# Six of the eight weight blocks of a shared expert's second half computed with seven block products instead of eight

## The reference

```
g, u   = split(x @ w_sh_gate_up)        # 512 -> 2 x 1024
shared = (silu(g) * u) @ w_sh_down      # 1024 -> 512
out    = layernorm(x + routed + shared)
```

## Time and profile before

| | us |
|---|---|
| median of 3 runs (lowest, highest) | 689.05 (688.68, 689.08) |
| the profiled execution's own time | 688.28 |
| its span | 686.5 |
| busy PE / DVE / ACT / POOL | 666.1 / 425.4 / 294.3 / 294.3 |

### The profile page before, as it was taken

The page is one execution under the profiler, slowest core; times in us unless marked ns, Lnnn a source line. Parts: engine busy times, 40 slices in busy tenths (PEclk is TensorE's granted clock), DMA queues, the critical chain, the costliest instruction groups (busy, mean ns, idle before and its releaser), DMA issues.

```text
span 686.5 us, 16409 instructions
## 1 busy us (share of the span) xinstructions
PE 666.1 (97%) x6828; PEld 531.9 (77%) x6828; DVE 425.4 (62%) x745; ACT 294.3 (43%) x510; POOL 294.3 (43%) x308
## 2 busy tenths in 40 slices
PE   9999999999999999999999999999999999999994
PEld 7767777677777777787887888888887888888883
DVE  5875865876844464488946544554456267676655
ACT  5343444455454432531023656655667442142232
POOL 0747567667645431011015335533552244726232
PEclk9999999999999999999999999999999999999998
DMA  8213234232642441100064478676748765414222
GB/s 286 83 35 86 76 98 106 88 112 57 175 138 75 129 141 33 46 0 1 21 231 157 140 292 295 214 220 255 216 153 271 229 218 159 123 66 131 65 78 92
DMA packets 65998, 92.47 MB, mean 135 GB/s; under 512 B 16960, under 2 KB 32064, under 8 KB 65920
## 3 DMA queue, kind: packets, MB, share of 16 engines
q1 hardware_dynamic: 60240, 72.76, 32.2%
q0 software_dynamic: 5680, 18.62, 9.4%
HBM read 67.56 MB, written 23.79 MB: 133 GB/s over the span
## 4 chain that ended last, share of the span: by engine, by line
PE 67%; DVE 14%; POOL 8%; issue 6%; ACT 4%; DMA 1%; POOLq 0%; DVEq 0%; ACTq 0%
PE zbank L1181 8%; PE wbank L1181 7%; PE bank L1305 7%; PE bank L1194 7%; PE bank L1073 7%; PE zbank L1268 6%; PE wbank L1268 6%; PE bank L1128 4%; DVE x L1464 3%; PE zbank L1281 2%; PE bank L1181 2%; PE wbank L1107 2%; PE zbank L1091 2%; POOL za L1758 2%; DVE sg L1454 1%
## 5 line engine op out<-in xcount | busy, mean ns | idle before, releaser
L1790 POOL TENSOR_TENSOR xl<-RAW,xh 128x1024 fp32r<-128x1024 f32 x23 | 55.4, 2407 | 121.1 <-ACT xh L1657 120.9
L1673 ACT ACTIVATE ah<-sg 128x512 fp32r<-128x512 f32 x48 | 30.3, 632 | 157.4 <-DVE sg L1454 157.4
L1803 POOL DMA_INDIRECT xg<-x1d,idxu x39 | 42.1, 1079 | 71.2 <-DVE idxu L889 41.3
L1444 DVE TENSOR_TENSOR GL<-RAW,GH 128x1024 fp32r<-128x1024 f32 x42 | 50.3, 1223 | 11.2 <-ACT GH L1652 9.8
L1456 DVE TENSOR_TENSOR al<-sg,ah 128x512 fp32r<-128x512 f32 x48 | 34.2, 712 | 33.5 <-ACT ah L1673 33.5
L1194 PE MATMUL bank<-xh,ah 128*128 128x512 f32 x128 | 51.3, 401 | 2.3 <-DVE x L1464 1.9
L1828 POOL DMA_INDIRECT xg<-yd,SI x32 | 35.8, 1120 | 40.0 <-DVE x L1512 23.6
L1194 PE MATMUL bank<-xh,al 128*128 128x512 f32 x128 | 50.0, 390 | 0.0
L1194 PE MATMUL bank<-xl,ah 128*128 128x512 f32 x128 | 49.9, 390 | 0.0
L1073 PE MATMUL bank<-xh,GH 128*128 128x512 f32 x112 | 47.9, 427 | 0.8 <-DVE kS L1346 0.8
L1454 DVE TENSOR_TENSOR sg<-sg,zbank 128x512 f32<-128x512 f32 x22 | 15.1, 685 | 53.4 <-PE zbank L1268 36.4
(11 more groups left out here) (301 smaller groups left out, 1753.6 us busy)
## 6 DMA issues: line engine op xcount, KB each, us to landing
RAW<-in_wgu SPq DMA_DIRECT2D x13, 1024.0 KB, 5.8
yd<-RAW SPq DMA_DIRECT2D x39, 256.0 KB, 5.2
RAW<-in_wsgu SPq DMA_DIRECT2D x14, 512.0 KB, 4.8
RAW<-in_wd SPq DMA_DIRECT2D x13, 512.0 KB, 5.8
xr<-in_xT SPq DMA_DIRECT2D x16, 256.0 KB, 4.7
x<-in_xtok SPq DMA_DIRECT2D x16, 256.0 KB, 4.2
x1d<-x SPq DMA_DIRECT2D x16, 256.0 KB, 2.5
RAW<-in_wsd SPq DMA_DIRECT2D x8, 512.0 KB, 4.5
```

The lines of the kernel that those rows point to most:

```text
L1444: e.tensor_tensor(GL[:, w % 2, k:k + 2, :], gate_raw(w, k), GH[:, w % 2, k:k + 2, :].bitcast(F32), ALU.subtract).then_inc(*mark("low", "g" ...
L1790: e.tensor_tensor(DL[:, w % 2, :, :], draw[:, raw_of(w), :, :], DH[:, w % 2, :, :].bitcast(F32), ALU.subtract).then_inc(*mark("low p", "d" ...
L1803: e.indirect_dma_start(place(s), None, x1d, bass.IndirectOffsetOnAxis(ap=idxu[:, LINES[s]:LINES[s] + 1], axis=0)).then_inc(*mark(f"dma xg{ ...
```

## The change

A unit half `fc` for the quarters 2 and 3 together is a product of a 2 x 2 block matrix of weights (gate and up; lower and upper half of the contraction) with a 2 x 2 block matrix of tokens (lower and upper half of the contraction; quarter 2 and quarter 3). The change computes six of the eight such products, numbered b = 2 to 7 (units BASE + 1 to BASE + 3), in Winograd's form of Strassen's method: seven block products of 6 matmuls each in place of eight. The two of unit BASE stay as they were.

The seven products need four sums of weight blocks for every b (`mix sums`, GpSimd, 128x256 each) and four sums of token blocks (`pair sums`, `pair more`: VectorE, 128x1024 each), all split into high and low again (`mix high`, `mix low`, `pair split`). The results are put together in PSUM: products accumulate onto each other, with three bank copies on ScalarE (`copy 1`, `copy 5`, `copy 2`) and two additions on VectorE (`add 5`, `add 7`) per b. PE's order in a block is 1, 5, 6, 2, 7, 3, 4, with four groups of a down (6 matmuls each) of the block before in between. Banks 0 to 3 are all in use by one block; the next one takes them over. The token fetch of quarter 3 is issued one job earlier than before, quarter 2 is fetched a second time (`fetch pair`), the routing's scratch memory is shared with it, and the last downs are (3, 3) and then (3, 2), with tiles 12 to 15 and 8 to 11 finished in these.

```diff
+SEVEN = {1: (0, "B11", 0, True), 2: (1, "B21", 0, False), 3: (6, "B22", 1, False), 4: (2, "T4", 2, False),
+         5: (3, "T1", 3, True), 6: (4, "T2", 1, False), 7: (5, "T3", 2, False)}
...
+    def mix(b, after):
+        do("mix sums", b, after)
+        do("mix high", b, after)
+        do("mix high sums", b)
+        do("mix low", b)
+    def block(b, order):
+        w, fc = BASE + b // 2, b % 2
+        for p in order:
+            do("mul", b, p, left[SEVEN[p][2]] if SEVEN[p][3] else None)
+            mul_end[b] = ("mul", b, p)
+            if p == 1:
+                do("copy 1", b, left[1])
+            elif p == 5:
+                do("copy 5", b)
+            elif p == 6:
+                do("copy 2", b, left[2])
+                do("add 5", b)
+            elif p == 2:
+                do("silu 2", b)
+                left[0] = ("silu", w, 2, fc)
+            elif p == 7:
+                do("add 7", b)
+            elif p == 3:
+                do("pair act", b, 3, ("down", w - 2, 3, 3) if b > 3 else None)
+                left[1], left[3] = ("silu", w, 3, fc), ("low", "a", w, 3, fc)
+            elif p == 4:
+                do("pair act", b, 2, ("down", w - 1, 2, 3))
+                left[2] = ("low", "a", w, 2, fc)
+            yield p
...
+        if j == JOBS - 3:
+            do("fetch pair")
+        if j == JOBS - 2:
+            do("fetch tokens", 3, ("gate", 4 + j, "r", 0, 1), range(4))
+        if j == JOBS - 1:
+            do("pair sums")
-        if j == JOBS - 1:
-            do("fetch tokens", 3, row_left[1], range(4))
...
-    seq = [(BASE + n, q) for n, q in ((0, 2), (0, 3), (1, 2), (1, 3), (2, 2), (3, 2), (2, 3), (3, 3))]
...
+    do("pair more", gate_end[4 + JOBS - 1])
+    rows_down(JOBS - 1, iter(()))
+    mix(2, gate_end[4 + JOBS - 1])
     do("fetch", 0)
     do("fetch", 1)
+    for step, _ in enumerate(first, 2):
+        if step < 6:
+            do("fetched high", 3, step - 2)
+            do("fetched low", 3, step - 2)
+    do("pair split", "T2", None)
+    split_down(BASE + 1)
+    do("load down", BASE + 2)
+    for step, _ in enumerate(gate(BASE, 3)):
+        if step % 2 == 0:
+            join(step // 2)
+    do("pair split", "T3", gate_end[BASE])
+    do("pair split", "T4", None)
+    join(4)
+    side = {(2, 3): "j5", (2, 4): "j6", (3, 1): "f0", (3, 3): "j7", (3, 4): "j8", (4, 1): "f1", (4, 5): "f2", (4, 3): "j9", (4, 4): "j10",
+            (5, 1): "f3", (5, 5): "f4", (5, 3): "j11", (5, 4): "j12", (6, 1): "f5", (6, 5): "f6", (6, 3): "j13", (6, 4): "j14",
+            (7, 1): "f7", (7, 3): "j15"}
+    for b in range(2, 8):
+        u = b // 2
+        downs = pair_down(u - 1, 2 + b % 2)
+        for p in block(b, (1, 5, 6, 2, 7, 3, 4)):
+            if p == 1 and b < 7:
+                after = mul_end[b - 1] if b > 2 else gate_end[BASE]
+                do("mix sums", b + 1, after)
+                do("mix high", b + 1, after)
+                if b in (4, 6):
+                    split_down(BASE + u)
+            if p == 2 and b < 7:
+                do("mix high sums", b + 1)
+                do("mix low", b + 1)
+            if p in (1, 3):
                 scale()
+            if (b, p) in side:
+                kind, i = side[b, p][0], int(side[b, p][1:])
+                (join if kind == "j" else finish)(i)
+            if p in (6 if b % 2 == 0 else 5, 2) or p in (3, 4) and b < 7:
+                next(downs, None)
+        if b == 2:
             do("load gate", BASE + 3)
             do("load down", BASE + 3)
+    scale()
+    for _ in downs:
+        pass
+    for i in pair_down(3, 3):
+        finish(i)
+        scale(keep=1)
+    for i in pair_down(3, 2):
...
+                elif step == "mul":
+                    b, p, free = a
+                    s, name, to, opens = SEVEN[p]
+                    if free:
+                        e.wait_ge(*on(*free))
+                    if p in (1, 2):
+                        e.wait_ge(*on("low", "m", b, 0))
+                    elif p == 4:
+                        e.wait_ge(*on("low", "m", b, 2))
+                    else:
+                        e.wait_ge(*on("low p", "m", b))
+                    if b == 2:
+                        e.wait_ge(*(on("low", "pair", name) if name[0] == "T" else on("low", "f", 3 if name == "B22" else 2, 3)))
+                    if p == 6:
+                        e.wait_ge(*on("copied", b, 1))
+                    elif p == 2:
+                        e.wait_ge(*on("copied", b, 1))
+                    elif p == 7:
+                        e.wait_ge(*on("copied", b, 2))
+                    elif p == 3:
+                        e.wait_ge(*on("added", b, 5))
+                    elif p == 4:
+                        e.wait_ge(*on("added", b, 7))
+                    for k in range(2):
+                        for wl, xlo in TERMS:
+                            t = e.matmul(bank[to][:], mixed(GL if wl else GH, b, s)[:, k, :], tokens_of(name, xlo)[:, k, :],
+                                         start=(opens and k == 0 and not wl and not xlo), stop=True, skip_group_check=True)
+                    t.then_inc(*mark("mul", b, p))
...
+                elif step == "pair sums":
+                    q1, q2, r1, r2 = pairs_[:, 0, :, :], pairs_[:, 1, :, :], XL1_[:, 0:2, :], XL1_[:, 2:4, :]
+                    e.wait_ge(*on("dma pair", 3))
+                    e.wait_ge(*on("dma xr1", 3, 3))
+                    e.tensor_tensor(q1, r1, q1, ALU.subtract).then_inc(*mark("pair sum", 1))
+                    e.tensor_tensor(q2, q2, r2, ALU.subtract).then_inc(*mark("pair sum", 0))
+                elif step == "pair more":
+                    gone, = a
+                    q1, q2, r1, r2 = pairs_[:, 0, :, :], pairs_[:, 1, :, :], XL1_[:, 0:2, :], XL1_[:, 2:4, :]
+                    e.wait_ge(*on(*gone))
+                    e.wait_ge(*on("pair sum", 0))
+                    e.tensor_tensor(RL_[:, 2:4, :], r2, q1, ALU.subtract).then_inc(*mark("pair sum", 2))
+                    e.tensor_tensor(q2, q2, q1, ALU.add).then_inc(*mark("pair sum", 4))
+                    e.wait_ge(*on("high", "pair", "T1"))
+                    e.tensor_tensor(tokens_of("T1", True), q1, tokens_of("T1", False).bitcast(F32), ALU.subtract).then_inc(*mark("low", "pair", "T1"))
+                    e.wait_ge(*on("low", "pair", "T1"))
+                    e.wait_ge(*on("pair sum", 4))
+                    e.tensor_tensor(q1, r2, r1, ALU.subtract).then_inc(*mark("pair sum", 3))
+                elif step == "pair split":
+                    name, gone = a
+                    raw = {"T2": RL_[:, 2:4, :], "T3": pairs_[:, 0, :, :], "T4": pairs_[:, 1, :, :]}[name]
+                    e.wait_ge(*on("high", "pair", name))
+                    e.tensor_tensor(tokens_of(name, True), raw, tokens_of(name, False).bitcast(F32), ALU.subtract).then_inc(*mark("low", "pair", name))
...
+                elif step == "pair split":
+                    name, gone = a
+                    raw = {"T2": RL_[:, 2:4, :], "T3": pairs_[:, 0, :, :], "T4": pairs_[:, 1, :, :]}[name]
+                    if gone:
+                        e.wait_ge(*on(*gone))
+                    if name == "T4":
+                        e.wait_ge(*on("low", "pair", "T3"))
+                    else:
+                        e.wait_ge(*on("pair sum", 3))
+                    e.activation(tokens_of(name, False), raw, ACT.Copy).then_inc(*mark("high", "pair", name))
+                elif step == "copy 1":
+                    b, free = a
+                    e.wait_ge(*on("mul", b, 1))
+                    e.wait_ge(*on(*free))
+                    e.activation(bank[1][:], bank[0][:], ACT.Copy).then_inc(*mark("copied", b, 1))
+                elif step == "copy 5":
+                    b, = a
+                    e.wait_ge(*on("mul", b, 5))
+                    if b > 2:
+                        e.wait_ge(*on("added", b - 1, 7))
+                    e.activation(turned[:], bank[3][:], ACT.Copy).then_inc(*mark("copied", b, 5))
+                elif step == "copy 2":
+                    b, free = a
+                    e.wait_ge(*on("mul", b, 6))
+                    e.wait_ge(*on(*free))
+                    e.activation(bank[2][:], bank[1][:], ACT.Copy).then_inc(*mark("copied", b, 2))
...
+                elif step == "mix sums":
+                    b, after = a
+                    e.wait_ge(*on(*gate_in(BASE + b // 2)))
+                    e.wait_ge(*on(*after))
+                    s1, s2, s3, s4 = (mixed(GL_, b, 3 + n) for n in range(4))
+                    e.tensor_tensor(s1, quarter(2, b), quarter(3, b), ALU.add).then_inc(*mark("mixed", b, 1))
+                    e.tensor_tensor(s3, quarter(0, b), quarter(2, b), ALU.subtract).then_inc(*mark("mixed", b, 3))
+                    e.wait_ge(*on("mixed", b, 1))
+                    e.tensor_tensor(s2, s1, quarter(0, b), ALU.subtract).then_inc(*mark("mixed", b, 2))
+                    e.wait_ge(*on("mixed", b, 2))
```

(13 more changed lines are left out.)

166 lines of the change are left out of this document (127 added, 39 removed).

## The result

The changed kernel takes 704.2 us (703.45 to 704.93), the kernel before 688.87 us (688.3 to 689.08) beside it: ratio 1.0224, 95% interval 1.0206 to 1.0242. That is slower, as forecast (697.2), but 0.2 us beyond the range's end of 704. The profiled execution took 703.45 us, its span is 701.7 us against 686.5. The last statistics end 15.15 us later, so the whole difference lies in this stretch.

The account below looks back on a forecast made before the run. PE was taken to bound the kernel. Saving 8.2 us, then adding 9.9 (block 2's start), 1 (clock), 3 (blocks 3 to 7) and 2.5 (tail) gave +8.2: median 697.2 us, range 686 to 704.

Parts of the forecast that it names:

- the waits of blocks 3 to 7: Blocks 3 to 7: late GpSimd sums, late copy 1 and VectorE-GpSimd meetings add 3 us, bounds 0 and 8.
- the clock: Start of block 2: the idle gap may halve PE's granted clock, adding 1 us, bounds nothing and 3.
- ahead of block 2: Before block 2: token sums fit VectorE's idle 9.59 us, joins 0 to 3 keep their times; nothing added, bounds 2 us either way.
- at its start: Block 2: product 5 waits 6.65 us for the multiplication, product 6 another 3.3 for copy 1; together 9.9 us.
- the tail: Behind PE's last matmul: eight tiles finished instead of four, 4.8 in place of 2.3 us; 2.5 more, bounds 1 and 3.5.
- the saving: Six block halves need 42 matmuls instead of 48 each; 36 matmuls at 0.227 us save 8.2 us of PE.
- The price of a meeting: When VectorE and GpSimd instructions meet at their shared port, it costs up to the length of the other instruction.
- The rival of the waiting blocks: Blocks wait on VectorE and GpSimd, about 1.5 us more each; +16.8 us at most, typically 702 to 706; chance 0.12.
- GpSimd's sum of 256 columns: GpSimd's weight sums in each block: price by width 0.77 us each, four sums 3.1 us together.

Follow-up runs that it names:

- the last version: The 686.4 us kernel (all reorderings, b = 2's low sums after quarter 3's last split) with finishes 0 to 7 one place later; 685.49 us, ratio 0.9982.
- the run with the start alone: Changed kernel with block 2's start reordered (copy 1 first, joins 3 and 4 later, b = 2's sums later), blocks 3 to 7 unchanged; 700.59 us, ratio 1.0181.
- the run at 688.83 us: Changed kernel with three reorderings in blocks 3 to 7 and block 2's start reordered (copy 1 first, joins 2 to 4 later); 688.83 us, ratio 1.0019.

## Why the prediction was wrong in size

The sum was 6.9 us short: 3.5 in the waits of blocks 3 to 7, 2.3 in the clock, 1.0 ahead of block 2, 0.4 at its start, and 0.3 too much in the tail. The mechanisms were the right ones; three terms were too small.

- **The direction, the place and the saving were right.** 36 matmuls at 0.227 us are 8.2 us; product 5 of block 2 waits for the late multiplication and product 6 for `copy 1`, in the order named, 10.3 us for 9.9 (VectorE's multiplication came 1.4 us later than before, and block 2 itself 1.0). That joins 2 and 3 hold it is shown by the run that moved them (7.0 to 0.6 us) and by the one that delayed their gathers (11.2 us).
- **"I take joins 0 to 3 at their old times, and nothing for this part"** was 1.0 us short. The 4.9 us of token sums were laid over VectorE's idle 9.59 us, but GpSimd's work in the same stretch was not laid beside them. The cover was there for VectorE's own durations, not for stretched ones: the first split of quarter 3's tokens took 2.41 us, and PE waited 1.3 us for one behind it. The run with the mixing of b = 2 later confirms it: 0.69 us, and block 2 starts 1.2 us earlier.
- **"I take 3 us for all of blocks 3 to 7"** is the step that failed most: 6.5 us. The waits for GpSimd were foreseen in blocks 5 and 7, at 1 us each; they were 2.0. That for `copy 1` was foreseen at 0.4 to 0.7 us in even blocks; it was 0.2 in block 4 and 1.0 in block 6. `mix low` was priced at 1.0 us on VectorE from the earlier trace rows; it took 2.5. (VectorE's terms also add up to 13.6 us, not the 13.4 that the prediction gives.) The price of a meeting, "up to the length of the other instruction", was right for one, but VectorE and GpSimd had been given the same place for work of the same step, so that they met in each block. The rival of the waiting blocks (first in the list) described this, with 0.12, and its 702 to 706 us hold the measurement. How the 6.5 us divide into the order of the queues and the meetings stays open: the two waits for GpSimd went when the low part of the down weights was moved, and also when the meetings were taken out, and each time waits for another engine came in their place.
- **The clock, 1 us,** was 3.3. The gap of 7 us did what was feared, and a second drop, in block 7, was not in the sum at all: it followed the second of the waits for GpSimd that had been taken at 1 us.
- **The tail** was 2.2 us for 2.5, **GpSimd's sum of 256 columns** 0.75 us for 0.77.
- **The Trainium skill**, SBUF — State Buffer, section "SBUF: two separate sides", calls the shared port pair an exclusive lock for a whole instruction. The trace agrees for one long instruction (2.41 us for a split of 0.69 beside GpSimd's 2.40), and for short ones in a row VectorE's 256-column split takes 0.957 us beside GpSimd's sums and 0.419 apart from them.

What stays open: why the runs of the last version spread over 7 us in two groups, and how far the waits left in blocks 2 and 3 can be ordered away.

## What to carry over

When matmuls are taken out, lay the other engines' queues side by side as they will be, not each against PE, and price every overlapping pair on VectorE and GpSimd as if the later one began when the earlier ended. A reordering that removes one wait often only shows the next one: judge it by when a group far behind starts, not by the wait. Work that waits for another engine belongs on a queue on which nobody's next step stands behind it.

## What the runs showed of the hardware

- A gap's length alone did not decide the granted clock. In the changed kernel it went to 0.50 at the gap of 7.0 us and at one of 2.0 us in block 7, while the gap of 2.0 us in block 5 left it at 1.00. The same wait of 2.0 us in block 5 took it to 0.50 in the run with `copy 1` first (630 to 632 us), and likewise in the run with joins 2 and 3 moved and in the one with the mixing of b = 2 later. And 3.65 us of waiting in the run with the start alone left it at 1.00 (windows):

```profile
607.00:611.00 4.00, 0.35 (x2) 0.26 (x2) 3.34 (x5) 1.45 (x3) 2.78 (x3) 1.00 0.52 94
611.00:614.00 3.00, 3.00 (x14) 2.45 (x14) 2.86 (x6) 2.40 (x5) 1.05 (x2) 1.00 0.79 313
```

- Both engines pay when they meet: from 545 to 552 us of the changed kernel VectorE's two instructions of 1024 columns took 1.76 and 1.64 us (1.22 alone), and GpSimd's sums of 256 columns 1.73, 1.72, 1.72 and 1.06 us (0.75 alone).
- A join (its gathered rows, weights and sum all in SBUF) is stretched as a split is: its two instructions took 3.79 us in place of 1.6 beside GpSimd's 2.40 us (the run at 688.83 us, from 645.88).
